# Scaling the off-diagonal product and adding the D term in one pass on VectorE

## The chip, the cores and the metric

The kernel runs on one core of a Trainium2 chip. The time is the device time of one execution in microseconds, and lower is better. The engines are TensorE (PE, with its weight loads PEld), VectorE (DVE), ScalarE (ACT), GpSimd (POOL) and SyncE (SP), which issues all DMAs.

## The reference

One block of a state-space layer with a small expert layer beside it, for 1024 tokens of width 512, in float32: `x = x + mamba(layernorm(x)) + moe(layernorm(x))`. The state-space part has 128 heads of 64 channels in 8 groups and works in chunks of 128 tokens:

```python
L = jnp.exp(_segsum(A_dt))
Y_diag = jnp.einsum('bzlhn,bzshn,bhzls,bzshp->bzlhp', Cc, Bc, L, xch)
...
Y_off = jnp.einsum('bzlhn,bzhpn,bhzl->bzlhp', Cc, prev, jnp.exp(A_cum))
Y = (Y_diag + Y_off).reshape(b, s, H, P) + hs * D[None, None, :, None]
g = y * jax.nn.silu(gate)
```

After that comes a normalisation within each group, a scale and the product with `out_proj_w`. What matters here is Y: for every token and head, the diagonal product, plus the product of C with the state carried into the chunk times `exp(A_cum)` (one factor for a token and a head), plus the convolved input `hs` times D (one factor for a head).

## The kernel before

The work is cut into 128 slots. Slot m is stage s = m // 8 (one of 16 sets of 8 heads, 512 channels) and chunk c = m % 8 (128 tokens, which are the 128 partitions). Two stages share a group's B and C, which are turned and multiplied in the even stages only. The state S of a stage runs through its eight chunks.

Every engine has a program written out by hand that goes through the slots in order; semaphores join them. Nothing is reordered at run time. Each matrix product in float32 is made of three, from operands split into a high and a low half (`xh`/`xl`, `GH`/`GL`, `SH`/`SL`, `gTh`/`gTl`, `OH`/`OL`).

TensorE in slot m: the front of slot m + 1 (L325 to L333, the turned B and the B by C product, in even stages), two, one or no halves of the input projection for the next stage (L265 to L267), Off(m) = C by state (L478 to L481, for c > 0), St(m) (L487 to L490), the output product O(m - 2) (L359 to L366), the diagonal product Y(m) (L502), the transposes of the gated result of m - 1 (L374), the gate's product for m + 1 (L342 to L349). O(m - 2) lies in PSUM bank 4, which the B product of m + 1 also uses in even stages: it has to wait until DVE has made the mask product Gt (L922) from it. Off(m) lies in bank 5, together with the transposes of m - 2, which L868 empties.

DVE in slot m: gate (L862), the scaled input dxh of m + 1 (L934), the blocks of m + 1 (L919, L922), the scaling of Off(m) (L1108), the state (L1115 or L1120), the convolution of a new tile (three L828) or the masked decays EM of m + 1 (L946) and silu of an old tile (L857), the output's accumulation (L891, L887), the sum into Y (L902), the gated product (L910), in slots with c = 1 the low half OL of the output weights (three L851), and gTl of slot m - 1 (L868). When there is a new tile, EM comes last.

POOL in slot m: xch of m + 1 (L1174), rstd of m - 2 (L1209 to L1213), the sum that is changed (L1263), then the front of m + 1: CL, SL (L1183), DL (L1186), the decay of S (L1189) and dhs, `hs` times D (L1198); then OL's fourth part (L1268), a low half for a store (L1163), a low half of weights (L1149) and a part of the output's accumulation (L1279). ACT copies high halves (SH with L659 right after S is updated), makes the decays (L606, L611), the tanh functions, and squares.

For c > 0 the Y of a slot is put together by two engines: DVE multiplies Off with the factors `SC[..., 1, :]`, broadcast over the 64 channels of a head, into a buffer (`yb` for even slots, `al[0]` for odd ones; `gated` is the pair). POOL adds dhs into the buffer. DVE adds the buffer to the Y bank at L902. The semaphore s_t1 counts the first, s_tp the second, s_t2 the third. There is one dhs buffer; POOL fills it for the next slot after its own sum. s_t1 also tells TensorE that the Off bank is free.

Of the kernel before, what the change touches and what calls it, by code (L numbers as in the profile page):

```python
# [6 lines left out]
def mamba_moe_block_kernel(nc, x, wa, wg, wo, wdt, cw, cbias, nw, dtb, alog, dvec, wbase, wrt, wla, wlb,  # L7
                           ident_c, tri_c, ex_c, out):
    f32, f32r, bf16, u32, u16 = (mybir.dt.float32, mybir.dt.float32r, mybir.dt.bfloat16, mybir.dt.uint32, mybir.dt.uint16)
    ALU, ACT, AX = mybir.AluOpType, mybir.ActivationFunctionType, mybir.AxisListType  # L10
# [51 lines left out]
    for m in range(M):  # L62
        c = m % 8
# [24 lines left out]
    def n7(m):  # L88
        return 7 * (m // 8) + m % 8 + 1

    def n0(m):
        return 7 * (m // 8) + m % 8
# [10 lines left out]
    def nsa(m):  # L103
        return 6 * (m // 8) + m % 8

    ctx = ExitStack()
    with ctx:
        def sb(name, shape, dt=f32):
            return ctx.enter_context(nc.sbuf_tensor(name, shape, dt))

        def sem(name):
            return ctx.enter_context(nc.semaphore(name))
# [19 lines left out]
        SC = [sb(f"SC{i}", [128, NC, 4, 8]) for i in range(2)]  # L132
# [7 lines left out]
        dhs = sb("dhs", [128, 512])  # L140
# [47 lines left out]
        gated, gates = (yb, al[0]), (tg, al[1])  # L188

        def decays(m):  # L190
# [31 lines left out]
        s_xch, s_dxh, s_dh, s_dl, s_dhs, s_sa, s_m, s_sl, s_sh = (  # L222
            sem(n) for n in ("xch_", "dxh_", "dh_", "dl_", "dhs_", "sa_", "m_", "sl_", "sh_"))
        s_gt, s_tg, s_sg, s_gtr, s_gth, s_gtl, s_sq, s_v, s_rst = (
            sem(n) for n in ("gtp", "tg_", "sg_", "gtr", "gth", "gtl", "sq_", "v_", "rst_"))
        s_stp, s_st, s_off, s_t1, s_tp, s_y, s_t2, s_g, s_o, s_pl, s_plr, s_alo, s_al, s_oh, s_ol = (
            sem(n) for n in ("stp", "st_", "offp", "t1", "tpl", "yp", "t2", "g_", "op", "pl_", "plr", "alo", "al_", "oh_", "ol_"))
        s_ts3, s_olp, s_gl3, s_mtl = (sem(n) for n in ("ts3", "olp", "gl3", "mtl"))

        te, se, ve, pe_, sp = nc.tensor, nc.scalar, nc.vector, nc.gpsimd, nc.sync  # L230
# [13 lines left out]
        def bank(kind, i):  # L244
            return P[:, at[kind, i][0], :]
# [47 lines left out]
        def bc(v):  # L293
            return v.unsqueeze(2).broadcast_to([128, 8, 64])

        def h8(t):
            return t.rearrange("p (h d) -> p h d", h=8)
# [596 lines left out]
        def dve_sum(m):  # L894
            c = m % 8
            y = gated[m % 2] if c else dhs
            ve.wait_ge(s_y, m + 1)
            if c:
                ve.wait_ge(s_tp, n0(m))
            else:  # L900
                ve.wait_ge(s_dhs, m + 1)
            ve.tensor_tensor(bank("Y", m), bank("Y", m), y[:, :], ALU.add).then_inc(s_t2, 1)  # L902
# [46 lines left out]
        def dve_program():  # L949
# [141 lines left out]
            for m in range(M + 2):  # L1091
                s, c = divmod(m, 8)
                new_tiles = [k // 2 for k in slot_halves[m + 1] if k % 2] if m < M else []
                old_tiles = [k // 2 for k in slot_halves[m] if k % 2] if m < M else []
                if 0 < m < M:
                    dve_gate(m)
                if m + 1 < M:
                    dve_scaled(m + 1)
                    dve_blocks(m + 1)
                if new_tiles:  # L1100
                    for i in old_tiles:
                        dve_silu(i)
                if m < M and c:
                    ve.wait_ge(s_off, n0(m))
                    if m > 1:
                        ve.wait_ge(s_gtr, m - 1)
                        ve.wait_ge(s_sq, m - 1)
                    ve.tensor_tensor(h8(gated[m % 2][:, :]), h8(bank("Off", m)), bc(SC[s % 2][:, c, 1, :]), ALU.mult).then_inc(s_t1, 1)  # L1108
                if c == 7 and s + 1 < NS:
                    dve_gate_lo(s + 1)  # L1110
                if m < M and c == 0:
                    ve.wait_ge(s_stp, n7(m))
                    if m:
                        ve.wait_ge(s_sl, n7(m) - 1)
                    ve.tensor_copy(S[:, :], bank("St", m)).then_inc(s_st, 1)  # L1115
                elif m < M and c != 7:
                    ve.wait_ge(s_stp, n7(m))
                    ve.wait_ge(s_sa, nsa(m))
                    ve.wait_ge(s_sl, n0(m))
                    ve.tensor_tensor(S[:, :], bank("St", m), S[:, :], ALU.add).then_inc(s_st, 1)  # L1120
                for i in new_tiles if m else ():
                    dve_conv(i)
                if not new_tiles and m + 1 < M:
                    dve_decay(m + 1)
                    for i in old_tiles:
                        dve_silu(i)
                if m >= 2:
                    dve_output(m - 2)
                if m == M - 1:
                    dve_gated_lo(m - 1)  # L1130
                if m < M:
                    dve_sum(m)
                    dve_gated(m)
                if m < M and c == 1:
                    dve_output_lo(s, (0, 1, 2))
                if m and m != M - 1 and m <= M:
                    dve_gated_lo(m - 1)
                for i in new_tiles if m == 0 else ():
                    dve_conv(i)
                if new_tiles and m + 1 < M:  # L1140
                    dve_decay(m + 1)
# [34 lines left out]
        def pool_front(m):  # L1176
            s, c = divmod(m, 8)
            if s % 2 == 0:
                pe_.wait_ge(s_ch, ngc(m))
                pe_.tensor_tensor(CL[:, tok(c)], Cx[:, tok(c)], as_f(CH[:, tok(c)]), ALU.subtract).then_inc(s_cl, 1)  # L1180
            if c:
                pe_.wait_ge(s_sh, n0(m))
                pe_.tensor_tensor(SL[:, :], S[:, :], as_f(SH[:, :]), ALU.subtract).then_inc(s_sl, 1)  # L1183
            if c != 7:
                pe_.wait_ge(s_dh, n7(m))
                pe_.tensor_tensor(DL[:, :], dxh[:, :], as_f(DH[:, :]), ALU.subtract).then_inc(s_dl, 1)  # L1186
            if 0 < c < 7:
                pe_.wait_ge(sc_in[s % 2], 32 * (s // 2 + 1))
                pe_.tensor_tensor(h8(S[:, :]), h8(S[:, :]), bc(EA[s % 2][:, :, c]), ALU.mult).then_inc(s_sa, 1)  # L1189
            if s:  # L1190
                pe_.wait_ge(ht_in[m % 2], 16 * (m // 2 - 3))
            else:
                pe_.wait_ge(s_hsr, m + 1)
            if m and (m - 1) % 8 == 0:
                pe_.wait_ge(s_t2, m)
            elif m:
                pe_.wait_ge(s_tp, n0(m - 1))
            pe_.tensor_tensor(h8(dhs[:, :]), h8(HT[m % 2]), bc(Dbc[:, 8 * s:8 * s + 8]), ALU.mult).then_inc(s_dhs, 1)  # L1198

        def pool_rstd(m):  # L1200
# [14 lines left out]
        def pool_program():  # L1215
# [30 lines left out]
            for m in range(M + 2):  # L1246
                s, c = divmod(m, 8)
                if m + 1 < M:
                    pool_scaled(m + 1)
                if m < M:  # L1250
                    if c == 0:
                        pe_.wait_ge(ts_in, 16 * (3 + 2 * s))
                        pe_.tensor_tensor(TS[:, 3, :], TS[:, 3, :], nwt[:, 4 * s + 3:4 * s + 4].broadcast_to([128, 512]),
                                          ALU.mult).then_inc(s_ts3, 1)
                    if c == 7 and s + 1 < NS:
                        pool_gate_lo(2 + s, (0, 1, 2))
                if m >= 2:
                    pool_rstd(m - 2)
                if m < M:
                    if c:  # L1260
                        pe_.wait_ge(s_t1, n0(m))
                        pe_.wait_ge(s_dhs, m + 1)
                        pe_.tensor_tensor(gated[m % 2][:, :], gated[m % 2][:, :], dhs[:, :], ALU.add).then_inc(s_tp, 1)  # L1263
                    if m + 1 < M:
                        pool_front(m + 1)
                    if c == 1:
                        pe_.wait_ge(s_oh, 4 * s + 1)
                        pe_.tensor_tensor(OL[:, 3, :], TS[:, 3, :], as_f(OH[:, 3, :]), ALU.subtract).then_inc(s_olp, 1)  # L1268
                    for k in slot_halves[m]:
                        if k % 2:  # L1270
                            pool_low_half(k // 2)
                    for k in slot_halves[m + 1]:
                        if k % 2:
                            pool_ring(k // 2 + 4)
                if m >= 2 and (m - 2) // 8 % 2 and (m - 2) // 8 < NS - 1:
                    n_, r, k = ngc(m - 2), m % 2, (m - 2) % 8
                    pe_.wait_ge(s_alo, n_)
                    pe_.wait_ge(s_plr, n_)
                    pe_.tensor_tensor(accS[:, k, :], accS[:, k, :], pl[r][:, :], ALU.add).then_inc(s_al, 1)  # L1279
# [191 lines left out]
```

## Time and profile before

| what | value |
|---|---|
| time, median of 3 runs | 1646.17 us (1645.4 to 1647.1) |
| the profiled execution, its own time | 1645.05 us |
| its span in the profile | 1643.7 us |
| TensorE busy, share of the span | 1607.2 us, 98% |
| DVE busy | 1384.0 us, 84% |
| POOL busy | 1332.3 us, 81% |
| ACT busy | 1240.3 us, 75% |
| L1108 on DVE, 112 times | 690 ns each |
| granted TensorE clock, mean | 0.997 of full speed |

The times of a row are microseconds from the start of the span; a mean of one instruction is in nanoseconds. "idle before" is how long an engine stood still just ahead of an instruction, with the one that ended the wait behind the arrow. "issue" means that the profile shows nothing it waited for. Matmuls follow each other in the pipeline, so the durations of neighbours overlap. The profile's 98% for TensorE is therefore read together with its idle times.

### The profile page before, as it was taken

What the parts mean: (1) busy time and instruction counts of PE and PEld (TensorE: products, weight loads), DVE (VectorE), ACT (ScalarE), POOL (GpSimd) and SP (SyncE); (2) the same over time, 40 slices, a digit from 0 to 9 for tenths busy, and PEclk for the clock granted to TensorE, in tenths of its full rate; (3) what the DMA queues carried; (4) which work ended last, traced back from release to release, by engine and by line L of the source; (5) the groups of instructions that cost most, each with busy time, mean ns of one, the idle gap of its engine ahead of it and who ended that gap; (6) DMA issues with size and microseconds to landing.
All of it is one profiled execution on the core that took longest, in us unless ns stands there. A gap on an engine that the chain in (4) does not pass through costs nothing.

```text
span 1643.7 us, 31884 instructions
## 1 busy us (share of the span) xinstructions
PE 1607.2 (98%) x10792; PEld 1301.3 (79%) x10792; DVE 1384.0 (84%) x1678; ACT 1240.3 (75%) x2628; POOL 1332.3 (81%) x1238
## 2 busy tenths in 40 slices
PE   7989999999999999999999999999999999999999
PEld 6777888878888788878888788887878788887777
DVE  5969789887989879897898878988798977989788
ACT  5267787787878787787877778687787878778775
POOL 3147689997889878897799968999688977999786
PEclk9999999999999999999999999999999999999999
DMA  4153356554644555454654536544563455534453
GB/s 128 66 199 102 108 169 178 161 155 126 187 124 137 160 154 145 122 153 126 188 146 141 140 116 190 142 138 142 153 173 103 139 154 170 167 117 145 117 161 104
DMA packets 216402, 236.13 MB, mean 144 GB/s; under 512 B 154280, under 2 KB 155824, under 8 KB 212016
## 3 DMA queue, kind: packets, MB, share of 16 engines
q1 hardware_dynamic: 216240, 234.08, 49.0%
q8 instruction: 88, 1.44, 0.4%
q14 instruction: 74, 0.61, 0.1%
HBM read 147.52 MB, written 55.05 MB: 123 GB/s over the span
## 4 chain that ended last, share of the span: by engine, by line
PE 71%; POOL 14%; DVE 9%; issue 6%; ACT 1%; DMA 0%; POOLq 0%; DVEq 0%; SPq 0%; ACTq 0%
PE P L265 8%; PE P L267 7%; PE P L266 7%; PE P L502 6%; PE P L359 5%; PE P L360 5%; PE P L342 5%; PE P L343 5%; PE P L349 5%; PE P L366 5%; PE P L374 3%; DVE OL L851 2%; POOL al L1263 2%; POOL GL L1154 2%; POOL hsX L1279 2%
## 5 line engine op out<-in xcount | busy, mean ns | idle before, releaser
L606 ACT ACTIVATE P<-AB,SC 128x128 f32<-128x128 f32 x1016 | 306.2, 361 | 16.1 <-DVE EM L946 16.0
L265 PE MATMUL P<-xh,AH 128*128 128x512 f32 x656 | 262.0, 399 | 2.8 <-DVE xl L977 2.1
L267 PE MATMUL P<-xh,AL 128*128 128x512 f32 x656 | 255.9, 390 | 0.0
L266 PE MATMUL P<-xl,AH 128*128 128x512 f32 x656 | 255.5, 389 | 0.0
L828 DVE SCALAR_TENSOR_TENSOR hsX<-P,cwt,hsX 128x1023 f32<-128x1023 f32 x189 | 241.8, 1279 | 13.1 <-ACT hsX L543 8.6
L342 PE MATMUL P<-GH,xh 128*128 128x512 f32 x512 | 212.3, 415 | 0.0
L359 PE MATMUL P<-OH,gTh 128*128 128x512 f32 x508 | 201.2, 396 | 10.3 <-DVE Gt L922 6.5
L343 PE MATMUL P<-GH,xl 128*128 128x512 f32 x512 | 201.3, 393 | 0.0
L360 PE MATMUL P<-OH,gTl 128*128 128x512 f32 x508 | 198.7, 391 | 0.0
L1149 POOL TENSOR_TENSOR AL<-AR,AH 128x512 fp32r<-128x512 f32 x82 | 109.9, 1341 | 81.0 <-ACT AH L530 81.0
L946 DVE TENSOR_TENSOR EM<-P,Gt 128x1024 f32<-128x1024 f32 x127 | 154.6, 1218 | 22.2 <-issue 22.0
L1186 POOL TENSOR_TENSOR DL<-dxh,DH 128x512 fp32r<-128x512 f32 x112 | 172.8, 1543 | 0.4 <-ACT DH L667 0.4
L1263 POOL TENSOR_TENSOR al<-al,dhs 128x512 f32<-128x512 f32 x64 | 97.8, 1529 | 85.7 <-DVE al L1108 85.7
L502 PEld LDWEIGHTS P<-xch,EM 128*64 128x64 f32 x4096 | 130.5, 138 | 45.2 <-issue 45.2
L1183 POOL TENSOR_TENSOR SL<-S,SH 128x512 fp32r<-128x512 f32 x112 | 152.4, 1361 | 17.0 <-ACT SH L659 15.8
L633 ACT ACTIVATE gTh<-P 128x512 fp32r<-128x512 f32 x127 | 75.7, 596 | 97.7 <-PE P L374 96.7
L502 PE MATMUL P<-xch,EM 128*64 128x64 f32 x4096 | 148.3, 226 | 0.0
L265 PEld LDWEIGHTS P<-xh,AH 128*128 128x128 f32 x656 | 123.4, 188 | 27.3 <-DVE xl L977 2.4
L267 PEld LDWEIGHTS P<-xh,AL 128*128 128x128 f32 x656 | 123.1, 188 | 26.8
L1174 POOL TENSOR_TENSOR xch<-hsX,SC 128x512 f32<-128x512 f32 x128 | 138.6, 1083 | 4.9 <-ACT hsX L585 2.9
L934 DVE TENSOR_TENSOR dxh<-hsX,SC 128x512 f32<-128x512 f32 x112 | 142.5, 1272 | 0.0
L266 PEld LDWEIGHTS P<-xl,AH 128*128 128x128 f32 x656 | 123.4, 188 | 23.6
(231 smaller groups left out, 4175.7 us busy)
## 6 DMA issues: line engine op xcount, KB each, us to landing
AB<-acr_d SPq DMA_DIRECT2D x128, 512.0 KB, 4.7
half_d<-hsX SPq DMA_DIRECT2D x60, 512.0 KB, 3.6
AR<-in_wa SPq DMA_DIRECT2D x80, 256.0 KB, 2.7
TS<-in_wg SPq DMA_DIRECT2D x16, 1024.0 KB, 6.1
TS<-in_wo SPq DMA_DIRECT2D x16, 1024.0 KB, 6.4
part_d<-pl SPq DMA_DIRECT2D x64, 256.0 KB, 3.3
pl<-part_d SPq DMA_DIRECT2D x64, 256.0 KB, 3.3
SC<-sct_d SPq DMA_DIRECT2D x16, 128.0 KB, 5.3
```

The lines of the kernel that those rows point to most:

```text
L265: te.matmul(o, ah_, bh_, start=(first and i == 0), stop=False)
L266: te.matmul(o, ah_, bl_, start=False, stop=False)
L267: r = te.matmul(o, al_, bh_, start=False, stop=(last and i == n - 1))
L342: te.matmul(o, xh[:, k, tok(c)], GH[:, k, :], start=n_ == 0, stop=False)
L343: te.matmul(o, xl[:, k, tok(c)], GH[:, k, :], start=False, stop=False)
L359: te.matmul(o, gTh[:, k, :], OH[:, k, :], start=k == 0, stop=False)
L360: te.matmul(o, gTl[:, k, :], OH[:, k, :], start=False, stop=False)
L502: r = te.matmul(o[f:f + 64, h * 64:(h + 1) * 64], EM[m % 2][:, at_ + f:at_ + f + 64], xch[m % 2][:, h * 64:(h + 1) * 64], start=True, stop ...
L606: r = se.activation(decays(m)[:, h, :], AB[m % 2][:, h, :], ACT.Relu, bias=SC[s % 2][:, c, 3, h:h + 1], scale=-1.0)
L828: ve.scalar_tensor_tensor(out=o[:, d:T], in0=raw[:, 0:T - d], scalar=cwt[:, n, 3 - d:4 - d], in1=o[:, d:T], op0=ALU.mult, op1=ALU.add).the ...
L946: ve.tensor_tensor(EM[m % 2][:, :].rearrange("p (h l) -> p h l", h=8), decays(m), Gt[:, c, :].unsqueeze(1).broadcast_to([128, 8, 128]), AL ...
L1186: pe_.tensor_tensor(DL[:, :], dxh[:, :], as_f(DH[:, :]), ALU.subtract).then_inc(s_dl, 1)
```

## The change

DVE no longer scales Off with one operation over all eight heads. It does eight, one for a head, over 64 columns. Each multiplies the head's 64 columns of the Off bank by the head's factor, taken as a scalar of each partition, and adds the same columns of dhs, and writes the buffer. POOL's sum of buffer and dhs (L1263) is gone, with its two waits and its semaphore s_tp. Three waits change with it: DVE waits for dhs before the eight; the sum into Y (L902) and POOL's next dhs wait for s_t1 in place of s_tp.

```diff
@@ dve_sum
             if c:
-                ve.wait_ge(s_tp, n0(m))
+                ve.wait_ge(s_t1, n0(m))
@@ dve_program, in the slot loop
-                    ve.tensor_tensor(h8(gated[m % 2][:, :]), h8(bank("Off", m)), bc(SC[s % 2][:, c, 1, :]), ALU.mult).then_inc(s_t1, 1)
+                    ve.wait_ge(s_dhs, m + 1)
+                    for h in range(8):
+                        cols = slice(64 * h, 64 * h + 64)
+                        r = ve.scalar_tensor_tensor(out=gated[m % 2][:, cols], in0=bank("Off", m)[:, cols],
+                                                    scalar=SC[s % 2][:, c, 1, h:h + 1], in1=dhs[:, cols], op0=ALU.mult, op1=ALU.add)
+                    r.then_inc(s_t1, 1)
@@ pool_front
             elif m:
-                pe_.wait_ge(s_tp, n0(m - 1))
+                pe_.wait_ge(s_t1, n0(m - 1))
             pe_.tensor_tensor(h8(dhs[:, :]), h8(HT[m % 2]), bc(Dbc[:, 8 * s:8 * s + 8]), ALU.mult).then_inc(s_dhs, 1)
@@ pool_program, in the slot loop
                 if m < M:
-                    if c:
-                        pe_.wait_ge(s_t1, n0(m))
-                        pe_.wait_ge(s_dhs, m + 1)
-                        pe_.tensor_tensor(gated[m % 2][:, :], gated[m % 2][:, :], dhs[:, :], ALU.add).then_inc(s_tp, 1)
                     if m + 1 < M:
                         pool_front(m + 1)
```

## Rows read from the trace of the kernel before

**Rows 1.** The page, busy time of each engine (us, share of the span, instructions)

```profile
PE 1607.2 (98%) x10792; PEld 1301.3 (79%) x10792; DVE 1384.0 (84%) x1678; ACT 1240.3 (75%) x2628; POOL 1332.3 (81%) x1238
```

**Rows 2.** Waits of all engines: who waited for whom, us in total, times, longest

```profile
POOL al L1263 <- DVE al L1108: 85.7, 40, 5.8
...
DVE P L902 <- POOL al L1263: 8.0, 14, 0.6
...
PE P L359 <- DVE Gt L922: 6.5, 8, 0.9
...
PE P L478 <- DVE gTl L868: 4.9, 8, 1.3
```

**Rows 3.** Line L1108: what its engine sat idle for (us, times)

```profile
  PE P L481: 121.2, 86
```

**Rows 4.** Timeline of TensorE: start, us, engine, operation, idle before and releaser

```profile
732.40 0.50 PE L359 MATMUL P<-OH,gTh 128*128 128x512 f32 x1 [0.84 <-DVE Gt L922]
...
827.29 0.50 PE L478 MATMUL P<-SH,CH 128*128 128x512 f32 x1 [0.51 <-DVE gTl L868]
```

**Rows 5.** Groups by line and form: xcount, busy us, mean ns, idle before

```profile
L1263 POOL TENSOR_TENSOR al<-al,dhs 128x512 f32<-128x512 f32 x64 | 97.8, 1529 | 85.7 <-DVE al L1108 85.7
...
L828 DVE SCALAR_TENSOR_TENSOR hsX<-P,cwt,hsX 128x1022 f32<-128x1022 f32 x63 | 80.8, 1282 | 2.2
...
L891 DVE SCALAR_TENSOR_TENSOR hsX<-P,rst,hsX 128x512 f32<-128x512 f32 x64 | 47.6, 744 | 4.6 <-PE P L366 2.6 <-PE P L518 1.6 <-DMA hsX<-acc_d 0.3
```

**Rows 6.** Timeline of VectorE before the slot loop

```profile
70.12 1.65 DVE L1065 TENSOR_SCALAR hsX<-hsX 128x128 f32<-128x128 f32 x8
```

**Rows 7.** Timeline of VectorE and POOL from slot 49 on (even stage)

```profile
719.08 0.69 DVE L1108 TENSOR_TENSOR al<-P,SC 128x512 f32<-128x512 f32 x1 [0.35 <-PE P L481]
...
721.50 1.22 DVE L857 SCALAR_TENSOR_TENSOR hsX<-th,hsX 128x1024 f32<-128x1024 f32 x1
...
721.52 2.34 POOL L1263 TENSOR_TENSOR al<-al,dhs 128x512 f32<-128x512 f32 x1
...
723.96 0.70 DVE L902 TENSOR_TENSOR P<-P,al 128x512 f32<-128x512 f32 x1 [0.58 <-POOL al L1263]
...
725.30 3.94 DVE L851 SCALAR_TENSOR_TENSOR OL<-TS,nwt,OH 128x512 fp32r<-128x512 f32 x3
...
729.17 0.68 DVE L868 TENSOR_TENSOR gTl<-P,gTh 128x512 fp32r<-128x512 f32 x1
...
731.87 0.28 DVE L919 TENSOR_TENSOR BL<-P,BH 128x128 fp32r<-128x128 f32 x1
...
732.07 0.28 DVE L922 TENSOR_TENSOR Gt<-P,tri 128x128 f32<-128x128 f32 x1
```

**Rows 8.** Timeline of VectorE and POOL in slot 57 (odd stage)

```profile
816.26 0.69 DVE L1108 TENSOR_TENSOR al<-P,SC 128x512 f32<-128x512 f32 x1 [1.03 <-PE P L481]
...
818.38 1.30 POOL L1183 TENSOR_TENSOR SL<-S,SH 128x512 fp32r<-128x512 f32 x1
...
818.68 2.08 DVE L857 SCALAR_TENSOR_TENSOR hsX<-th,hsX 128x1024 f32<-128x1024 f32 x1
...
822.09 4.54 DVE L851 SCALAR_TENSOR_TENSOR OL<-TS,nwt,OH 128x512 fp32r<-128x512 f32 x3
...
826.55 0.68 DVE L868 TENSOR_TENSOR gTl<-P,gTh 128x512 fp32r<-128x512 f32 x1
```

**Rows 9.** Timeline of VectorE in slot 51

```profile
743.66 0.69 DVE L1108 TENSOR_TENSOR al<-P,SC 128x512 f32<-128x512 f32 x1 [1.41 <-PE P L481]
```

**Rows 10.** Busy us of each engine in sixteen slots, and in the last stage

```profile
core 0: us, PE busy (x) PEld busy (x) DVE busy (x) ACT busy (x) POOL busy (x), PEclk, DMA share, GB/s
250.00:443.00 193.00, 191.65 (x1308) 155.78 (x1307) 165.33 (x195) 152.00 (x322) 166.69 (x154) 1.00 0.54 156
1602.00:1629.00 27.00, 26.83 (x204) 21.48 (x203) 25.33 (x32) 18.84 (x46) 25.48 (x30) 1.00 0.41 111
```

**Rows 11.** Timeline of VectorE in slot 1

```profile
133.22 1.22 DVE L946 TENSOR_TENSOR EM<-P,Gt 128x1024 f32<-128x1024 f32 x1 [0.52 <-issue]
```

More of the change, by code:

```diff
@@ L225, in mamba_moe_block_kernel @@
             sem(n) for n in ("gtp", "tg_", "sg_", "gtr", "gth", "gtl", "sq_", "v_", "rst_"))
-        s_stp, s_st, s_off, s_t1, s_tp, s_y, s_t2, s_g, s_o, s_pl, s_plr, s_alo, s_al, s_oh, s_ol = (
-            sem(n) for n in ("stp", "st_", "offp", "t1", "tpl", "yp", "t2", "g_", "op", "pl_", "plr", "alo", "al_", "oh_", "ol_"))
+        s_stp, s_st, s_off, s_t1, s_y, s_t2, s_g, s_o, s_pl, s_plr, s_alo, s_al, s_oh, s_ol = (
+            sem(n) for n in ("stp", "st_", "offp", "t1", "yp", "t2", "g_", "op", "pl_", "plr", "alo", "al_", "oh_", "ol_"))
         s_ts3, s_olp, s_gl3, s_mtl = (sem(n) for n in ("ts3", "olp", "gl3", "mtl"))
```

## The prediction

> **What bounds the kernel now.** I read the page first [rows 1]: TensorE (PE) is busy 98% of the span, the other three 75 to 84%. Such a kernel gets slower only where TensorE is made to wait. So I next read the waits of all engines [rows 2]. The reader is to see how short TensorE's list is. Its two largest waits in the slot loop are both for VectorE (DVE), of eight times each: 6.5 us for the mask product of L922 and 4.9 us for the low half gTl of L868. The changed instruction itself, L1108, found TensorE's Off product unready 86 times, 121 us in all [rows 3]. DVE thus has slack in most slots and none in a few.
>
> The timeline of TensorE says which few [rows 4]. The pattern repeats every 16 slots (two stages s, 193 us). TensorE stops 0.84 us in slot c = 2 of the even stages (before L359, for L922) and 0.51 us in slot c = 2 of the odd ones (before L478, for L868). Both follow slot c = 1, the one in which DVE also makes OL with three instructions of L851. The late chain is then: L1108 of slot c = 1, S, the masks, silu, L902, L910, three L851, L868 (there the odd stage stops), L862, L934, L919, L922 (there the even one stops). I went through slots 49 (even stage) and 57 (odd) instruction by instruction [rows 7, 8]. Elsewhere DVE catches up by waiting: in slot 51 L1108 itself starts after 1.41 us of idleness [rows 9].
>
> **The change part by part.**
>
> *Removed from POOL:* 112 sums (L1263), the 64 on al of 1.53 us in the mean [rows 5], with the waits before them. Neither of TensorE's waits in [rows 2] is for POOL, so this alone gives TensorE nothing. What DVE gains is its wait at L902 for POOL: 14 times, 0.57 us each [rows 2], one of them in slot 49 (0.58 us before L902 [rows 7]), none in slot 57.
>
> *Removed from DVE:* 112 times L1108, 0.69 us by itself [rows 7]; the next instruction follows 0.60 us after it when nothing is waited for (estimate: 0.69 less the 0.08 by which neighbours overlap in slot 49, where L919 starts at 731.87 and lasts 0.28 and L922 starts at 732.07 [rows 7]).
>
> *Added to DVE:* eight operations of 128x64, PSUM and one SBUF tensor in, scalar from SBUF. None is in the trace. Same form, wider: L891 with 512 columns takes 0.744 us, L828 with 1022 columns 1.282 us [rows 5]. That is 1.055 ns a column, so 64 columns take 0.744 - 448 x 0.00106 = 0.27 us. With the overlap of 0.08 taken off, eight narrow ones start 0.19 us apart: 8 x 0.194 = 1.55 us. The one run of eight short operations with such a scalar agrees: eight L1065 fill 1.65 us [rows 6]; with the last one as long as the 0.28 of L919, (1.65 - 0.28) / 7 = 0.196 us from start to start. The bounds: below, two-tensor operations without such a scalar are 0.20 us apart at 128 columns (L919, L922) and so 0.20 - 64 x 0.00106 = 0.133 us at 64, 8 x 0.133 = 1.07 us; above, if none overlapped its neighbour, 8 x 0.27 = 2.17 us. So a slot costs DVE 0.95 us more (bounds 0.47 and 1.57). I take the middle, since two forms with the same kind of scalar meet there.
>
> The Trainium skill bears on the upper bound ("VectorE: DVE Perf Modes", section "The DRAIN you can't avoid"): the next operation is said not to start until the pipeline of the one before is empty. By it the eight would cost their full durations, the upper bound, and the sum would be that of the third case below. This trace speaks against it: L922 starts 0.08 us before L919 is over [rows 7].
>
> *Moved waits.* L1108 now waits for dhs too. POOL makes dhs one iteration ahead of the sum, and at the sum POOL stood idle for L1108 40 times on al alone [rows 2]: dhs was long there. I price it at 0; with that cover gone it would be about one POOL operation, 1.5 us. POOL may overwrite dhs and TensorE the Off bank only after the last of the eight, 0.95 us later; in TensorE's order the bank's next user, the transposes, comes after the whole of O and Y. The S update of L1120 stands behind the eight on DVE, so SH, SL and the next Off product's operands come up to 0.95 us later; that product is a slot away (193 / 16 = 12 us), and POOL no longer has a sum in front of SL. These are 0.
>
> *Does DVE have the room?* Over sixteen slots it is busy 165.3 of 193 us [rows 10]; 14 of the 16 slots get 0.95 us, 13.3 of the 27.7 free. In most slots the next wait for TensorE swallows it. In slots c = 1 it does not.
>
> What the operations collide with is a term of its own. L891 and L828, one SBUF tensor and PSUM, fit one line of 1.055 ns a column, with no time lost to POOL in the mean [rows 5]; the new form is the same, so I let POOL and the eight run free of each other.
>
> *Slot c = 1, odd stages (slot 57).* The idle time before L1108 is ahead of the eight and can't absorb them. Behind it DVE runs without a gap to L868, for which TensorE already waits. So the stop grows by 0.95 us. Seven such stages in the regular part (s = 1 to 13): 6.7 us.
>
> *Slot c = 1, even stages (slot 49).* +0.95, less 0.58 of waiting for POOL at L902, = +0.37. But a second thing goes with POOL's sum. In slot 49 silu (L857) took 1.22 us and POOL's sum, started 0.02 us later, took 2.34; in slot 57 L857 started 0.30 us after POOL's SL (L1183) and took 2.08 [rows 7, 8]. In these rows whichever starts first runs at its own speed and the other waits for it. With the sum gone, slot 49 looks like slot 57: SL starts as soon as SH is there, 0.3 us ahead of L857. So L857 loses 2.08 - 1.22 = 0.86 us, and the three L851 meet POOL as in slot 57, 4.54 instead of 3.94, +0.60. Sum: 0.37 + 0.86 + 0.60 = 1.83 us, in seven stages (s = 2 to 14) 12.8 us.
>
> *Head.* Slot 1 has 0.52 us of idleness before L946 [rows 11], behind L1108: 0.95 - 0.52 = +0.4 us on the stops of slot 2.
>
> *Tail.* From 1602 to 1629 us, about three slots of the last stage, DVE is busy 25.33 of 27 us [rows 10]: 3 x 0.95 - 1.67 = 1.2 us, and the last slot about 0.8 more: 2 us.
>
> **Sum:** 0.4 + 6.7 + 12.8 + 2 = 21.9 us, on the profiled execution's 1645.05: 1667 us. That execution lies 1.1 us below the median, less than the sum can tell; I leave it at 1667.
>
> **The rivals.**
>
> *The collision does not move (chance 0.22).* If L857 still wins in slot 49, each even stage costs 0.37: 0.4 + 6.7 + 2.6 + 2 = 11.7, 1657 us. The operations at the lower bound come to about the same: 0 + 7 x 0.47 + 7 x 1.35 + 0.8 = 13.6, 1659. For it: the outcome hangs on 0.3 us. Against it: both SL and L857 follow from the same S update, so their distance should be that of slot 57.
>
> *The eight do not overlap (0.15).* +1.57 a slot: head 1.0, odd 11.0, even 7 x 2.45 = 17.2, tail 3 x 1.57 - 1.67 + 1.5 = 4.5: 33.7, 1679 us. For it: durations of 0.27 us. Against: the spacing of neighbours [rows 6, 7].
>
> *Faster: POOL's relief frees DVE (0.07).* The three L851 of slot 57 are 1.5 us each [rows 8] where L891, as wide, takes 0.744 [rows 5]: they lose some 2.2 us to POOL in each c = 1 slot. Should POOL's work fall elsewhere, L868 would come earlier and both stops vanish: at most 6.5 + 4.9 = 11.4 us, 1634. It decides once more than 0.95 us (odd) or 0.37 us (even) of such losses go in slot c = 1. Against it: what stands behind the sum on POOL's queue and so overlaps L851, DL, S, dhs and OL, all stays; the sum was over (721.52 + 2.34) before L851 began [rows 7].
>
> *No change within 0.2% (0.06).* The lateness would have to be absorbed in c = 1, by operations at the lower bound and no moved collision: 3.3 + 0.8 = 4, 1649. The 0.2%, 3.3 us, is what a measurement of this kernel can tell from nothing.
>
> **How the numbers follow.** The forecast case has 0.50, at 1667. 1654 to 1681 takes it, the second and the third case in, with a few us for each; about 0.83. Faster 0.07, same 0.06, slower 0.87.
>
> **What would show it.** DVE busy up by 112 x (8 x 0.27 - 0.69) = 165 us in summed durations, although the path pays 0.95 a slot; POOL down by its 112 sums, some 160 us. The stops of TensorE in slot c = 2 near 1.5 us (odd) and 2.7 us (even), in the same two places, nowhere new. L857 of slot 49 at about 2.1 us. L902 no longer waiting for POOL. L1108's waits for TensorE shorter by about as much as the eight are longer, since DVE arrives later. Wrong would be: stops in other slots, DVE waiting for dhs, or even-stage stops at 1.2 us.

## The result and the profile after

The changed kernel takes 1666.02 us (median, 1665.04 to 1666.7), the kernel before on the same chip 1645.79 us: ratio 1.0119, interval 1.0107 to 1.0131, so 20 us slower. The profiled execution took 1665.87 us, its span is 1664.6 us.

The page of the changed kernel, busy time of each engine, beside [rows 1]:

```profile
PE 1607.5 (97%) x10792; PEld 1300.6 (78%) x10792; DVE 1485.4 (89%) x2462; ACT 1242.5 (75%) x2628; POOL 1201.9 (72%) x1126
```

TensorE does the same work in the same time; only its pauses grew. DVE is busy 101 us more, POOL 130 us less. The waits of the changed kernel, beside [rows 2] (who waited for whom, us in total, times, longest):

```profile
POOL SL L1188 <- ACT SH L659: 316.6, 105, 6.9
ACT SH L659 <- DVE S L1125: 115.2, 93, 3.0
...
PE P L478 <- DVE gTl L868: 17.8, 15, 1.4
...
PE P L359 <- DVE Gt L922: 10.0, 15, 0.9
```

POOL now waits 317 us in front of SL. It was relieved, and nothing used the relief. TensorE's two waits for DVE grew from 4.9 to 17.8 and from 6.5 to 10.0 us, and each from 8 to 15 times. The timeline of TensorE over one period of sixteen slots, beside [rows 4], shows where:

```profile
704.02 0.50 PE L359 MATMUL P<-OH,gTh 128*128 128x512 f32 x1 [0.51 <-DVE Gt L922]
...
738.08 0.50 PE L478 MATMUL P<-SH,CH 128*128 128x512 f32 x1 [0.98 <-DVE gTl L868]
...
740.57 0.50 PE L359 MATMUL P<-OH,gTh 128*128 128x512 f32 x1 [0.84 <-DVE Gt L922]
...
836.31 0.50 PE L478 MATMUL P<-SH,CH 128*128 128x512 f32 x1 [1.35 <-DVE gTl L868]
```

In the odd stage the stop of 0.51 us became 1.35. In the even one the 0.84 is unchanged, and a second stop of 0.98 stands ahead of it. The one at 704.02 is new: slot 47, c = 7 of an odd stage.

The eight operations and what follows them in slot 49 of the changed kernel, beside [rows 7] (timelines of DVE and POOL; behind the change the new kernel's line numbers are 3 to 5 higher):

```profile
726.21 1.63 DVE L1111 SCALAR_TENSOR_TENSOR al<-P,SC,dhs 128x64 f32<-128x64 f32 x8 [0.44 <-PE P L481]
...
727.75 0.68 DVE L1125 TENSOR_TENSOR S<-P,S 128x512 f32<-128x512 f32 x1
...
729.18 1.28 POOL L1188 TENSOR_TENSOR SL<-S,SH 128x512 fp32r<-128x512 f32 x1 [1.41 <-ACT SH L659]
...
729.48 2.07 DVE L857 SCALAR_TENSOR_TENSOR hsX<-th,hsX 128x1024 f32<-128x1024 f32 x1
...
732.13 0.68 DVE L902 TENSOR_TENSOR P<-P,al 128x512 f32<-128x512 f32 x1
...
733.46 3.96 DVE L851 SCALAR_TENSOR_TENSOR OL<-TS,nwt,OH 128x512 fp32r<-128x512 f32 x3
...
737.34 0.68 DVE L868 TENSOR_TENSOR gTl<-P,gTh 128x512 fp32r<-128x512 f32 x1
```

The eight fill 1.63 us, 1.54 from the first to what follows. L902 has no wait for POOL. L857 takes 2.07 us where it took 1.22, because SL started 0.30 us ahead of it. From the scaling's start to L868 are 11.13 us, against 729.17 - 719.08 = 10.09 before: +1.04. Three steps make it up. In the kernel before, the state's update followed the one scaling after 0.68 us, so the eight add 1.54 - 0.68 = 0.86. L857 and what follows it add 0.86. From L891 to L902 it is 0.66 us where it was 1.33, which takes off 0.67. The lines for that, first those of the kernel before (timelines of DVE):

```profile
719.76 0.69 DVE L1120 TENSOR_TENSOR S<-P,S 128x512 f32<-128x512 f32 x1
...
722.63 0.75 DVE L891 SCALAR_TENSOR_TENSOR hsX<-P,rst,hsX 128x512 f32<-128x512 f32 x1
```

```profile
731.47 0.74 DVE L891 SCALAR_TENSOR_TENSOR hsX<-P,rst,hsX 128x512 f32<-128x512 f32 x1
```

A recorded stop understates what it costs. It begins at the modelled end of the matmul before, and matmuls of 512 columns last 0.39 us but start 0.23 us apart; the first one behind the stop at 704.02 lasts 0.50 us, and the next starts 0.34 us after it. So I also took the length of a slot: from the first matmul of Y (L502) of one slot to that of the next, in the timeline of TensorE. Worked out so for sixteen slots (44 to 60) of each profiled execution, in us; the slots not shown are equal within 0.02 in all of them:

```
slot (c)          47 (7)  48 (0)  50 (2)  51 (3)  58 (2)  59 (3)   sum of 16
before             10.92   11.22   12.98   11.60   12.04   13.96     193.34
changed            11.74   10.93   14.04   11.60   12.88   13.95     195.76
e1_only_c1         10.92   11.25   14.02   11.60   12.88   13.95     195.25
e2_all_but_c1      11.72   10.92   11.66   11.61   12.06   13.96     192.56
e3_wide_no_sum     10.93   10.93   13.16   11.60   12.03   13.95     193.23
e4_eight_pool_sum  11.78   10.92   13.31   11.61   12.87   13.96     195.07
e5_four_wide       11.76   10.93   13.51   11.61   12.39   13.95     194.78
e6_before_reord.   10.92   11.21   11.60   11.61   11.24   13.95     191.16
e7_after_reord.    11.73   10.93   11.61   12.69   11.23   14.90     193.70
e8_silu_first      11.76   10.93   13.33   11.61   12.16   13.96     194.37
e10_both_orders    11.72   10.93   11.60   12.94   11.24   14.40     193.47
e11_blocks_first   10.93   11.15   11.61   12.91   11.23   14.37     192.82
e12_ol_ahead       10.93   11.16   11.60   12.95   11.23   14.22     192.72
```

The change costs 2.42 us in sixteen slots: 1.06 in slot 50, 0.84 in slot 58, 0.82 in slot 47, less 0.29 in slot 48. Before the change slot 48 held a stop that no wait recorded. It is gone in every run in which slot 47 has its stop, and also in e3, where slot 47 has none. In the row of e2, slot 50 is an exception, as told below. Six periods measured together, slots 19 to 115, agree: 193.38 before, 195.77 after. The last stages (slot 115 to the end) cost 3.0 us more.

### The profile page after: what moved, and what is told of

It is laid out like the page before. It is cut to its first block, busy times and chain, and to the rows that moved or that the text cites. A ratio compares the mean times of both kernels' runs of the same rounds, so it can differ in the third digit from the quotient of the medians.

```text
span 1664.6 us, 32556 instructions
## 1 busy us (share of the span) xinstructions
PE 1607.5 (97%) x10792; PEld 1300.6 (78%) x10792; DVE 1485.4 (89%) x2462; ACT 1242.5 (75%) x2628; POOL 1201.9 (72%) x1126
## 4 chain that ended last, share of the span: by engine, by line
PE 78%; DVE 14%; issue 4%; ACT 3%; DMA 0%; DVEq 0%; POOL 0%; SPq 0%; ACTq 0%; POOLq 0%
PE P L265 8%; PE P L267 8%; PE P L266 8%; PE P L502 7%; PE P L359 6%; PE P L342 6%; PE P L360 6%; PE P L366 6%; PE P L349 6%; PE P L343 6%; PE P L374 4%; DVE OL L851 3%; DVE EM L946 2%; ACT P L606 2%; DVE hsX L828 1%
## 5 line engine op out<-in xcount | busy, mean ns | idle before, releaser
L1188 POOL TENSOR_TENSOR SL<-S,SH 128x512 fp32r<-128x512 f32 x112 | 144.3, 1288 | 317.4 <-ACT SH L659 316.6
L828 DVE SCALAR_TENSOR_TENSOR hsX<-P,cwt,hsX 128x1023 f32<-128x1023 f32 x189 | 241.9, 1280 | 13.1 <-ACT hsX L543 8.6
L1191 POOL TENSOR_TENSOR DL<-dxh,DH 128x512 fp32r<-128x512 f32 x112 | 183.6, 1639 | 7.9 <-ACT DH L667 7.9
L502 PEld LDWEIGHTS P<-xch,EM 128*64 128x64 f32 x4096 | 130.5, 138 | 45.3 <-issue 45.3
L659 ACT ACTIVATE SH<-S 128x512 fp32r<-128x512 f32 x112 | 70.9, 633 | 115.5 <-DVE S L1125 115.2
L946 DVE TENSOR_TENSOR EM<-P,Gt 128x1024 f32<-128x1024 f32 x127 | 154.3, 1215 | 1.7 <-issue 1.5
L1179 POOL TENSOR_TENSOR xch<-hsX,SC 128x512 f32<-128x512 f32 x128 | 151.5, 1184 | 4.1 <-ACT hsX L585 2.4
L1203 POOL TENSOR_TENSOR dhs<-hsX,Dbc 128x512 f32<-128x512 f32 x128 | 148.5, 1160 | 1.9 <-DVE P L902 1.9
L502 PE MATMUL P<-xch,EM 128*64 128x64 f32 x4096 | 148.3, 226 | 0.0
L349 PE MATMUL P<-GL,xh 128*128 128x512 f32 x512 | 138.3, 392 | 0.0
```

What stands on the lines that cost most here:

```text
L349: r = te.matmul(o, xh[:, k, tok(c)], GL[:, k, :], start=False, stop=n_ == 3)
L502: r = te.matmul(o[f:f + 64, h * 64:(h + 1) * 64], EM[m % 2][:, at_ + f:at_ + f + 64], xch[m % 2][:, h * 64:(h + 1) * 64], start=True, stop ...
L828: ve.scalar_tensor_tensor(out=o[:, d:T], in0=raw[:, 0:T - d], scalar=cwt[:, n, 3 - d:4 - d], in1=o[:, d:T], op0=ALU.mult, op1=ALU.add).the ...
L946: ve.tensor_tensor(EM[m % 2][:, :].rearrange("p (h l) -> p h l", h=8), decays(m), Gt[:, c, :].unsqueeze(1).broadcast_to([128, 8, 128]), AL ...
```

## The experiments

All were timed in three rounds beside the kernel before; the ratio is to that.

**One pass only in slots c = 1.**

```diff
-                    (eight operations in every slot with c > 0)
+                    if m % 8 == 1:
+                        (eight operations, as in the changed kernel)
+                    else:
+                        ve.tensor_tensor(h8(gated[m % 2][:, :]), h8(bank("Off", m)), bc(SC[s % 2][:, c, 1, :]), ALU.mult).then_inc(s_t1, 1)
```

POOL's sum with its waits is there in the same slots as the wide operation.

> One pass (eight operations on DVE) only in the 16 slots with c = 1; in the other 96 DVE scales with one operation and POOL sums, as before. Theory (the loss sits in slots c = 1, the only ones where DVE has no slack behind the operation): about 13 us of the 20 us come with these 16 slots, plus 1 us in the first stage: 1660 us, with TensorE's stops in slots c = 2 as after the full change (1.36 us odd, 1.82 us even) and none in slots c = 7. Rival (the loss is DVE's load in general, in proportion to the slots changed): 16/112 of 20 us, 1649 us.

Measured: 1661.32 us, ratio 1.0095 (1.0078 to 1.0112), 15 of the 20 us. Slots 50 and 58 are as after the full change, slot 47 as before it. One seventh of the edit carries three quarters of the loss.

**One pass everywhere but in slots c = 1.** The same edit with `m % 8 != 1`.

> The reverse: one pass in the 96 slots with c = 2 to 7, and in the 16 slots with c = 1 the single scaling on DVE and the sum on POOL, as before. Theory: TensorE's stops in slots c = 2 as before the change (0.5 and 0.84 us), the new stop of 0.5 us in slots c = 7 of odd stages stays (3.5 us over seven stages), the last stage costs about 2.5 us: 1652 us. Rival (load in general): 96/112 of 20 us, 1663 us.

Measured: 1647.72 us, ratio 1.0011 (1.0001 to 1.0020). 96 slots get the slower form and it costs 1 to 2 us, less than I expected: slot 47 does grow by 0.80 us and the last stages by 1.9, but slot 48 gives back 0.30, and so do the slots c = 2 of the even stages. There the table's slot 50, with 1.3 us less, is not typical. The same slot of the six other even stages from slot 18 to slot 114 takes 12.55 to 12.60 us, where it took 12.96 to 13.04 before: 0.4 us less. With slot 50 they give back 3.9 us in all. By this the two halves of the edit, 15 and 1 us, do not add up to its 20. From the timelines of POOL and DVE in slots 49 and 50, and behind them the same place one period earlier, in slot 34:

```profile
720.74 1.30 POOL L1282 TENSOR_TENSOR al<-al,dhs 128x512 f32<-128x512 f32 x1
...
724.15 0.70 DVE L911 TENSOR_TENSOR P<-P,al 128x512 f32<-128x512 f32 x1
...
730.52 1.59 POOL L1180 COPY hsX<-hsX 128x1024 uint16<-128x1024 uint16 x1
730.54 0.68 DVE L943 TENSOR_TENSOR dxh<-hsX,SC 128x512 f32<-128x512 f32 x1
731.14 0.28 DVE L928 TENSOR_TENSOR BL<-P,BH 128x128 fp32r<-128x128 f32 x1
```

```profile
537.10 1.04 POOL L1180 COPY hsX<-hsX 128x1024 uint16<-128x1024 uint16 x1
537.12 1.57 DVE L943 TENSOR_TENSOR dxh<-hsX,SC 128x512 f32<-128x512 f32 x1
```

POOL, relieved in the slots ahead, does its sum in 1.30 us where it took 2.34 [rows 7], and L911 (L902 before) doesn't wait for it. So POOL's relief was worth 0.4 us in each even stage. The rest of slot 50's gain is chance. POOL's copy and L943 (L934 before), the scaled input ahead of the blocks, start within 0.02 us of each other both times; in slot 50 L943 goes first and takes 0.68 us, in slot 34 the copy does and L943 takes 1.57. The recorded starts do not tell which of the two wins.

**POOL's sum gone, one wide scaling.** This kernel leaves the D term out of Y for c > 0.

```diff
-                    for h in range(8):
-                        (scalar_tensor_tensor of head h)
-                    r.then_inc(s_t1, 1)
+                    ve.tensor_tensor(h8(gated[m % 2][:, :]), h8(bank("Off", m)), bc(SC[s % 2][:, c, 1, :]), ALU.mult).then_inc(s_t1, 1)
```

> DVE scales with one wide operation as before, and POOL's sum is gone: the D term is left out of Y in the slots with c > 0 (dhs is still computed and DVE still waits for it). This is the removal on POOL by itself. Theory: in even stages, slot c = 1, DVE no longer waits 0.58 us for POOL but its silu L857 loses 0.86 us to POOL's SL, +0.3 us in seven stages: 1648 us, within 1646 to 1650. Rival A (POOL's relief frees DVE, the eight operations alone cost): faster than before, 1640 us or less. Rival B (the moved collisions carry the loss): 1655 us or more.

Measured: 1644.87 us, ratio 0.9992 (0.9982 to 1.0002): no change. L857 in slot 49 takes 2.07 us here too, on the timeline of DVE:

```profile
720.61 2.07 DVE L857 SCALAR_TENSOR_TENSOR hsX<-th,hsX 128x1024 f32<-128x1024 f32 x1
```

So taking the sum away is what moves the collision, and the wait at L902 that it saves pays for most of it: slot 50 grew by 0.18 us, slot 48 shrank by 0.29.

**Eight scalings, POOL's sum kept.**

```diff
-                    ve.tensor_tensor(h8(gated[m % 2][:, :]), h8(bank("Off", m)), bc(SC[s % 2][:, c, 1, :]), ALU.mult).then_inc(s_t1, 1)
+                    for h in range(8):
+                        cols = slice(64 * h, 64 * h + 64)
+                        r = ve.tensor_scalar(gated[m % 2][:, cols], bank("Off", m)[:, cols], SC[s % 2][:, c, 1, h:h + 1], None, ALU.mult)
+                    r.then_inc(s_t1, 1)
```

> The eight narrow operations by themselves: DVE scales with eight operations of 64 columns (no sum in them), POOL's sum stays. Theory: these cost 0.95 us a slot as in the full change, POOL's sum adds nothing in odd stages; stops in slots c = 2 of 1.36 us (odd) and about 1.6 us (even), 0.5 us in c = 7 of odd ones: about 1663 us. Rival (POOL's absence is what costs): 1650 us or less.

Measured: 1660.56 us, ratio 1.0088 (1.0072 to 1.0105). Adding D in the same operation costs nothing: 273 ns a piece against 276, and 1.54 us from the first to what follows in both. The count of operations does. Slot 58 is as after the full change; slot 50 is 0.73 us shorter. There L857 takes 1.34 us (L857 in slot 49, timeline of DVE), since POOL's sum stands before SL again:

```profile
728.48 1.34 DVE L857 SCALAR_TENSOR_TENSOR hsX<-th,hsX 128x1024 f32<-128x1024 f32 x1
```

**Four operations of 128 columns.** Each uses its first head's factor for two heads, so Y is another one.

```diff
-                    for h in range(8):
-                        cols = slice(64 * h, 64 * h + 64)
+                    for h in range(0, 8, 2):
+                        cols = slice(64 * h, 64 * h + 128)
```

> The changed kernel with four operations of 128 columns instead of eight of 64; each uses the factor of its first head for two heads, so Y is another one. Theory (a fixed 0.13 us for each operation is what the eight cost): four start 0.26 us apart, 1.04 us in all, 0.44 us more than the single scaling instead of 0.95. TensorE's stops in slots c = 2 shrink by 0.5 us each, the 0.5 us stop in c = 7 goes: 1653 us. Rival (the added D term or the scalar operand costs by element, not by operation): the same as with eight, 1666 us.

Measured: 1654.89 us, ratio 1.0053 (1.0037 to 1.0070). The four, from the timeline of DVE in slot 49:

```profile
721.67 1.13 DVE L1111 SCALAR_TENSOR_TENSOR al<-P,SC,dhs 128x128 f32<-128x128 f32 x4 [0.45 <-PE P L481]
722.71 0.68 DVE L1125 TENSOR_TENSOR S<-P,S 128x512 f32<-128x512 f32 x1
```

1.04 us from the first to what follows, against 1.54 for eight: four operations fewer save 0.50 us, 0.125 us each, over the same 512 columns. Slots 50 and 58 shrink by 0.53 and 0.49. The stop in slot 47 did not go, though I had expected it to; slot 47 is as long as with eight. DVE's timeline from the scaling of slot 46 to L922 in slot 47 shows why. First the kernel before, then the changed kernel, then this one:

```profile
685.49 0.69 DVE L1108 TENSOR_TENSOR yb<-P,SC 128x512 f32<-128x512 f32 x1 [2.24 <-PE P L481]
...
694.83 0.88 DVE L934 TENSOR_TENSOR dxh<-hsX,SC 128x512 f32<-128x512 f32 x1
...
695.83 0.28 DVE L922 TENSOR_TENSOR Gt<-P,tri 128x128 f32<-128x128 f32 x1
```

```profile
692.09 1.63 DVE L1111 SCALAR_TENSOR_TENSOR yb<-P,SC,dhs 128x64 f32<-128x64 f32 x8 [2.24 <-PE P L481]
...
702.37 1.19 DVE L934 TENSOR_TENSOR dxh<-hsX,SC 128x512 f32<-128x512 f32 x1
...
703.69 0.28 DVE L922 TENSOR_TENSOR Gt<-P,tri 128x128 f32<-128x128 f32 x1
```

```profile
687.52 1.13 DVE L1111 SCALAR_TENSOR_TENSOR yb<-P,SC,dhs 128x128 f32<-128x128 f32 x4 [2.23 <-PE P L481]
...
697.30 1.69 DVE L934 TENSOR_TENSOR dxh<-hsX,SC 128x512 f32<-128x512 f32 x1
...
699.11 0.28 DVE L922 TENSOR_TENSOR Gt<-P,tri 128x128 f32<-128x128 f32 x1
```

From the scaling's start to the end of L922 are 10.62, 11.88 and 11.87 us. The four save 0.50 us, and L934 loses the same 0.50 again: POOL's three GL operations started 0.65 us ahead of it in the changed kernel and 0.16 us ahead of it here, so it waits longer for the first of them. In the kernel before they started behind it, and it took 0.88 us.

**The three L851 spread, in both kernels.**

```diff
                     dve_blocks(m + 1)
+                if m < M and c == 2:
+                    dve_output_lo(s, (1, 2))
@@ behind dve_gated(m)
-                if m < M and c == 1:
-                    dve_output_lo(s, (0, 1, 2))
                 if m and m != M - 1 and m <= M:
                     dve_gated_lo(m - 1)
+                if m < M and c == 1:
+                    dve_output_lo(s, (0,))
```

> The kernel before, with DVE's three L851 put elsewhere: one after gTl (L868) in slot c = 1, two after the blocks (L922) of slot c = 2. Theory (TensorE's two stops in each sixteen slots are DVE's lateness behind the three L851): both stops go, some 10 us: 1636 us. Rival (the stops only move, O(m-2) then waits for OL): 1645 us or more.

> The changed kernel with the same reordering. Theory: the change costs only where DVE has no slack, so the stops in c = 2 (1.36 and 1.82 us) go and the 0.5 us in c = 7 of odd stages stays, as do some 3 us of the last stage: 1644 us, about 8 us over the reordered kernel before. Rival (the change costs whatever the order): 20 us over the reordered kernel before.

Measured: the kernel before with this order takes 1627.80 us, ratio 0.9889 (0.9873 to 0.9906), 18 us less, more than the recorded stops; slots 50 and 58 fall to 11.60 and 11.24. It is the fastest version of the study. The changed kernel with it takes 1651.21 us, ratio 1.0025 (1.0015 to 1.0035), which is 23 us above the reordered kernel before. Here the rival's number came: the change costs as much as in the old order. But not in all slots; apart from slot 47's the stops have moved to slots c = 3. The timelines of DVE and TensorE in slots 50 and 51 of the changed, reordered kernel:

```profile
736.22 2.82 DVE L851 SCALAR_TENSOR_TENSOR OL<-TS,nwt,OH 128x512 fp32r<-128x512 f32 x2
738.96 1.61 DVE L1113 SCALAR_TENSOR_TENSOR yb<-P,SC,dhs 128x64 f32<-128x64 f32 x8
740.50 0.67 DVE L1127 TENSOR_TENSOR S<-P,S 128x512 f32<-128x512 f32 x1
741.09 3.90 DVE L828 SCALAR_TENSOR_TENSOR hsX<-P,cwt,hsX 128x1023 f32<-128x1023 f32 x3
...
745.05 0.50 PE L265 MATMUL P<-xh,AH 128*128 128x512 f32 x1 [0.19 <-DVE hsX L828]
```

The kernel before in the same order, at the same place:

```profile
726.06 3.90 DVE L828 SCALAR_TENSOR_TENSOR hsX<-P,cwt,hsX 128x1023 f32<-128x1023 f32 x3
...
731.52 0.48 PE L265 MATMUL P<-xh,AH 128*128 128x512 f32 x1
```

L851 and the eight now both stand ahead of the convolution, whose banks TensorE wants. In the kernel before it is over 1.6 us before TensorE comes (729.96 against 731.52). In the changed one it ends 1.9 us later, counted from the Y of slot 50. In slots 49 and 50 the eight add 0.87 and 0.93 us, L857 behind SL 0.84, and L934, which takes 1.18 us instead of 0.69, another 0.5; DVE's waits, of 0.58, 0.35 and 0.22 us there and 0.19 in all here, take off about 1. This stop is about half of what slot 51 grew by; the rest lies further on in the slot, where two matmuls start late (748.70, 749.76), the second right behind the end of L922 at 749.70. (The profiled execution of e7 lost some 4 us ahead of slot 1 and is above its own median; slot lengths leave that out.)

**silu ahead of the masks in slots c = 1, in the changed kernel.**

```diff
-                    dve_decay(m + 1)
+                    if c != 1:
+                        dve_decay(m + 1)
                     for i in old_tiles:
                         dve_silu(i)
+                    if c == 1:
+                        dve_decay(m + 1)
```

> The changed kernel with silu (L857) ahead of the masked decays (L946) in slots c = 1, so that it is over before POOL's SL can start. Theory (L857 and SL exclude each other): L857 takes 1.2 us instead of 2.07, stops in c = 2 shrink by 0.85 us in each stage: 1654 us. Rival (the slower L857 is not the cause of the stops): 1666 us.

Measured: 1655.81 us, ratio 1.0057 (1.0039 to 1.0075). L857 takes 1.21 us in slot 49, and slots 50 and 58 shrink by 0.71 and 0.72 us. With L857 out of SL's way 10 of the 20 us are gone; this is a mending of both stages' collisions, of which the odd one was there before the change.

**Three more orders of the changed kernel.** e10 has both reorderings, e11 also makes the blocks (L919, L922) before L934 in slots c = 7, e12 also puts the one L851 of slot c = 1 ahead of L868.

```diff
+                    if c == 7:
+                        dve_blocks(m + 1)
                     dve_scaled(m + 1)
-                    dve_blocks(m + 1)
+                    if c != 7:
+                        dve_blocks(m + 1)
```

> The changed kernel with both reorderings: L851 split (one after L868, two in slot c = 2) and silu ahead of the masked decays in slots c = 1. With L851 split alone, the stops moved to slots c = 3 (1.1 us longer in even stages, 0.9 in odd), where the input projection waits for the convolution. Theory (DVE is late by the sum of what stands ahead in slots c = 1 and 2; silu gives back 0.85 us of it): these stops shrink to about 0.3 and 0.1 us, sixteen slots take 192.0 us instead of 193.7: 1639 us. Rival (silu's time is not on the path to the convolution): 1651 us.

> As e10, and in slots c = 7 DVE makes the blocks (L919, L922) before the scaled input (L934). Theory (the new stop of slots c = 7 in odd stages is TensorE waiting for L922, which stands 1.2 us behind L934 on DVE): slot 47 takes 10.9 us again instead of 11.7, sixteen slots 191.2: 1633 us. Rival (L922 is late for another reason): as e10.

> As e11, with the one L851 of slot c = 1 ahead of L868 instead of behind it. In e10 and e11 silu's 0.85 us did not come through: L868 then stood idle 1.04 us for ACT's high half gTh (L633), and the L851 behind it was late by as much. Theory (that wait took the gain): the L851 fills the wait, slot 51 takes about 11.9 us instead of 12.9 and slot 59 about 14.0 instead of 14.4: some 9 us less than e11, 1636 us. Rival (the stop in slots c = 3 comes from DVE's load in slot c = 2 alone): as e11, 1645 us.

Measured: 1648.60 us (ratio 1.0015, 1.0005 to 1.0025), 1644.73 us (0.9995, 0.9985 to 1.0005) and 1645.08 us (0.9994, 0.9985 to 1.0004). The theory's number was missed all three times; the rival of e12 had the right one. What e11 was to show of slot 47 came, though: with the blocks ahead, slot 47 takes 10.93 us, so its stop was TensorE waiting for L922 behind L934. What silu saved did not come through in the even stages: slot 51 takes 12.94 us instead of 12.69, while slot 59 takes 14.40 instead of 14.90. In e10 L868 of slot 49 waited 1.04 us for gTh; e12 filled that wait. The two timelines, first e10's of DVE, then e12's of DVE and POOL:

```profile
729.83 0.67 DVE L862 SCALAR_TENSOR_TENSOR tg<-tg,P 128x512 f32<-128x512 f32 x1
730.42 0.92 DVE L934 TENSOR_TENSOR dxh<-hsX,SC 128x512 f32<-128x512 f32 x1
```

```profile
726.76 0.93 DVE L851 SCALAR_TENSOR_TENSOR OL<-TS,nwt,OH 128x512 fp32r<-128x512 f32 x1
727.87 0.69 DVE L868 TENSOR_TENSOR gTl<-P,gTh 128x512 fp32r<-128x512 f32 x1 [0.18 <-ACT gTh L633]
729.30 0.69 DVE L862 SCALAR_TENSOR_TENSOR tg<-tg,P 128x512 f32<-128x512 f32 x1 [0.74 <-ACT tg L651]
729.80 1.03 POOL L1176 COPY hsX<-hsX 128x1024 uint16<-128x1024 uint16 x1
729.90 1.47 DVE L934 TENSOR_TENSOR dxh<-hsX,SC 128x512 f32<-128x512 f32 x1
...
731.70 2.83 DVE L851 SCALAR_TENSOR_TENSOR OL<-TS,nwt,OH 128x512 fp32r<-128x512 f32 x2
734.46 1.61 DVE L1116 SCALAR_TENSOR_TENSOR yb<-P,SC,dhs 128x64 f32<-128x64 f32 x8
735.99 0.67 DVE L1130 TENSOR_TENSOR S<-P,S 128x512 f32<-128x512 f32 x1
736.59 3.90 DVE L828 SCALAR_TENSOR_TENSOR hsX<-P,cwt,hsX 128x1023 f32<-128x1023 f32 x3
```

Counted from the Y of slot 49 (723.62 us in e10, 723.66 in e12), L862 does start 0.57 us earlier in e12, now waiting for tg, which TensorE and ACT make. Then L934 meets POOL's copy, which started 0.10 us ahead of it, and takes 1.47 us instead of 0.92. With that the gain is gone, and the convolution starts where it did. So the rival's number came, but not for the rival's reason in the even stages: what DVE won ahead of tg it lost to POOL behind it. From tg to the end of the convolution are 736.59 + 3.90 - 729.30 = 11.2 us without a gap, against 729.96 - 720.50 = 9.5 in e6; the eight are 0.92 of the difference and L934 is 0.78 (1.47 for 0.69). None of these orders beats the reordered kernel before, 1627.80 us.

## Why the prediction was right

It said 1667 us, it was 1666. The mechanism held in the slots that it named, but it missed a third place, and its total is nearer than its terms, which is luck. By its terms, each from the slot lengths (head and tail from the same timelines):

- *The eight operations.* 8 x 0.194 = 1.55 us was predicted, 1.54 measured to the next start; 0.27 us each, 0.276 measured. They overlap, so the third case falls, and the fixed part of 0.125 us an operation is shown by e5. The other form (e4) costs the same. One of the two grounds for 1.55 was none: the eight L1065 are 128 columns wide, and operations of the new form with 128 columns start 0.26 us apart (e5), not 0.196. The other ground, L891 and L828 with the overlap taken off, gave the right number.
- *Odd stages.* +0.95 us was predicted, +0.84 measured, seven times: 5.9 for 6.7. The single scaling was taken to hold up what follows it for 0.60 us; in slots c = 1 it was 0.68 (719.08 to 719.76, and the same in slot 57).
- *Even stages.* +1.83 was predicted, +1.06 measured, 7.4 for 12.8. The step that was mis-sized is L851 meeting POOL "as in slot 57, 4.54 instead of 3.94": it took 3.96. L891 stands between L857 and L851 in slot 49 and not in slot 57, so the three start later in POOL's sequence. The first L851 started 0.21 us after POOL's decay of S in slot 57 of the kernel before and 0.80 us after it in slot 49 of the changed one, and had 0.84 and 0.26 us left to wait for its end: a difference of 0.58 us, as 4.54 - 3.96. The timelines of POOL, first before, then changed:

```profile
821.88 1.05 POOL L1189 TENSOR_TENSOR S<-S,EA 128x512 f32<-128x512 f32 x1
```

```profile
732.66 1.06 POOL L1194 TENSOR_TENSOR S<-S,EA 128x512 f32<-128x512 f32 x1
```

- *L857 behind SL.* This part of the even stages, 0.86 us, came to 0.85, and e3, e4 and e8 show it: present whenever the sum is gone and silu is behind the masks, 1.34 us with the sum back.
- *A stop that was missed.* "Nowhere new" was wrong, and stops in other slots were among the signs of being wrong that the prediction named. In slot 47 L922 stands behind L934 and is over 1.26 us later after the scaling of slot 46 than before the change, 0.93 by the eight and 0.31 because L934 took 1.19 us for 0.88. TensorE came for it 0.6 us after its end before the change (696.11, 696.74): +0.82 in slot 47, and e11, with the blocks ahead of L934, takes it away. Slot 48 gives back 0.29; together seven times 3.7 us. I had looked for margins only in the slots in which TensorE waited already.
- *Head and tail.* 0.4 was predicted, and slot 2 grew by 0.60; another 0.5 us lie ahead of the first Y, before any changed operation, and are not of the change. 2.0 predicted for the tail, 3.0 measured. The new stop and these nearly cancel the missing 5.4 us of the even stages.
- *POOL.* Its relief by itself is worth nothing (e3), as predicted; that it is worth 0.4 us in each even stage where DVE keeps the single scaling in c = 1 (e2) I had not seen. Its busy time fell by 130 us and not by 160, since its other operations got slower, DL for one from 1.54 to 1.64 us in the mean.
- *DVE busy.* +165 us of summed durations was predicted and is 112 x 8 x 0.275 - 77 = 169; the page shows 101, because it counts overlapping operations once.
- *DVE's waits.* It never waited for dhs, as predicted. Its wait for Off fell from 121.2 to 85.3 us, by 36 and not by the some 100 that the eight are longer; its waits at other lines took part of the rest, such as L946 (22.0 to 1.5 us) and L862.

"Only in slots c = 1" holds for this order of DVE's program (e1 against e2), not in general: in the reordered kernel the lateness met the convolution in c = 2 (e7), and cost as much. What stays open is what decides between DVE and POOL when both start within 0.02 us, as in e2, and with it how much of the change's cost in another order is the eight operations and how much is the meetings with POOL that they shift.

## What to carry to other kernels

An engine with 16% of idle time can have none in two slots of sixteen, and what is added costs there alone; so walk the period slot by slot and write down, for each thing the bounding engine takes from the edited one, how early it is ready, in the slots without a wait too. Replacing one operation over eight groups with eight operations pays the fixed part seven times more (0.125 us each here); merging a second operand into them was free. Work taken off a relieved engine also moves its next operation, here into a collision of 0.85 us where the work itself had caused a wait of 0.58. Such collisions can eat a saving whole: L934 took back the 0.50 us that four operations fewer saved ahead of slot 47 (e5) and 0.55 us of e12's gain. And look first at what else stands in the tight slot: spreading the three L851 gained 18 us.

## What the runs showed of the hardware

DVE's silu L857, with two inputs in SBUF, took 1.2 us when it started before POOL's operation and 2.07 when SL was under way, while POOL's next one took 2.28 instead of 1.3: in these rows they took turns, in whole operations. L934, SBUF alone, took 0.68 to 1.81 us by where it met POOL. With starts 0.02 us apart now the one and now the other went first (e2). The new operations, one input in PSUM and one in SBUF, kept to 266 to 286 ns in all 896 cases whatever POOL did. A stop recorded as 0.51 us lengthened slot 47 by 0.82 us, and slot 48 before the change lost 0.29 us with no stop recorded.
